# Three operands of VectorE's work in a 512-step recurrence are placed in PSUM instead of SBUF

## What is computed

```python
h = silu(cond @ W1.T + b1); gate = sigmoid(h @ W2.T + b2)
x = x + (x + x * gate)                 # layer 0: the transform and its inverse cancel, so x1 = x * (2 + gate)
# layer 1: a recurrence over the 512 steps
h_t = tanh(x1[:, t] @ Wx + b + h_{t-1} @ Wh);   x2[:, t] = x1[:, t] + h_t
# layer 2, from x2
f, i = sigmoid(x2 @ Wf.T + bf), sigmoid(x2 @ Wi.T + bi)
s = f + i + EPS;  f, i = f / s, i / s;  n = i * (x2 @ Wh2.T + bh)
# decays and cumulative sums of f and n over time, added to x2, give x3
# layer 3, from x3: for each batch a rank-8 correction (from cond) of a base matrix
out = x3 + x3 @ (x3-independent matrix of this batch)
```

## Time and profile before

| | us |
|---|---|
| runs | 1658.1, 1659.96, 1660.72; median 1659.96 |
| profiled execution, whole / span of the core | 1663.04 / 1661.2 |
| busy: PE, PEld | 1498.4 (90%), 1152.1 (69%) |
| busy: DVE, ACT, POOL | 1138.5 (69%), 556.5 (34%), 695.7 (42%) |

### The profile page before, as it was taken

How to read it: one execution, slowest core, us unless ns; L and a number is a source line. 1 busy time by engine, 2 the same in 40 slices (tenths; PEclk the granted TensorE clock), 3 DMA queues, 4 the chain that set the end, 5 groups by cost and what they waited for, 6 DMA issues and landing times. The chain is left out here.

```text
span 1661.2 us, 48465 instructions
## 1 busy us (share of the span) xinstructions
PE 1498.4 (90%) x20708; PEld 1152.1 (69%) x20708; DVE 1138.5 (69%) x2722; ACT 556.5 (34%) x1606; POOL 695.7 (42%) x540
## 2 busy tenths in 40 slices
PE   4768999999999999999999999999987976989998
PEld 3435777777777777777777777777776754666666
DVE  4223576776768676767677776768676778898884
ACT  3313333333333334333333333333323322232322
POOL 1314243434334444434343434434334447565563
PEclk9678999999999999999999999999997997999999
DMA  7263032424142323323232324142234367777672
GB/s 297 89 233 136 9 66 49 69 40 84 26 80 39 67 46 59 53 55 61 51 63 52 68 39 84 27 78 40 40 75 122 85 116 204 259 242 265 233 260 79
DMA packets 443114, 167.74 MB, mean 101 GB/s; under 512 B 407906, under 2 KB 411106, under 8 KB 439571
## 3 DMA queue, kind: packets, MB, share of 16 engines
q1 hardware_dynamic: 442898, 164.64, 39.5%
HBM read 96.25 MB, written 68.16 MB: 99 GB/s over the span
## 5 line engine op out<-in xcount | busy, mean ns | idle before, releaser
L437 PEld LDWEIGHTS recb<-hs,scanS 128*128 128x128 f16 x16384 | 444.7, 96 | 245.6 <-DVE hs L1087 237.2
L437 PE MATMUL recb<-hs,scanS 128*128 128x32 f16 x16384 | 495.8, 177 | 70.7 <-DVE hs L1087 68.7
L622 ACT ACTIVATE hs<-pre 128x64 f16<-128x64 f32 x512 | 131.6, 257 | 824.1 <-DVE pre L1079 824.1
L1077 DVE TENSOR_TENSOR pre<-recb,xw 128x64 f32<-128x64 f32 x512 | 114.7, 224 | 256.7 <-PE recb L437 255.3
L1087 DVE TENSOR_TENSOR hs<-hbuf,hs 128x64 f16<-128x64 f32 x512 | 170.1, 332 | 147.1 <-ACT hbuf L623 145.3
L947 DVE RECIPROCAL gates<-gates 128x64 f32<-128x64 f32 (+1 forms) x484 | 258.7, 555 | 0.4
L810 POOL TENSOR_TENSOR xt<-xt,hbuf 128x512 f32<-128x512 f32 x64 | 100.0, 1562 | 207.9 <-ACT hbuf L623 207.9
L798 POOL TENSOR_TENSOR x1lo<-xt,x1hi 128x512 fp32r<-128x512 f32 x62 | 87.7, 1416 | 219.1 <-ACT x1hi L629 211.5
L814 POOL TENSOR_TENSOR gates<-gates 128x512 f32<-128x512 f32 x64 | 83.1, 1299 | 174.0 <-DVE gates L947 174.0
L823 POOL TENSOR_TENSOR xt<-xt,pout 128x512 f32<-128x512 f32 x64 | 76.3, 1192 | 188.4 <-DVE pout L973 188.4
L1079 DVE TENSOR_TENSOR pre<-recb,pre 128x64 f32<-128x64 f32 x512 | 115.0, 225 | 17.6
(11 more groups left out here) (194 smaller groups left out, 2780.3 us busy)
## 6 DMA issues: line engine op xcount, KB each, us to landing
xt<-in_x SPq DMA_DIRECT2D x64, 256.0 KB, 3.4
g_d<-gst SPq DMA_DIRECT2D x64, 256.0 KB, 4.1
n_d<-nst SPq DMA_DIRECT2D x64, 256.0 KB, 3.0
x_d<-xt SPq DMA_DIRECT2D x64, 256.0 KB, 3.1
out<-gates SPq DMA_DIRECT2D x64, 256.0 KB, 2.5
xt<-x_d SPq DMA_DIRECT2D x28, 512.0 KB, 5.4
stage<-in_w SPq DMA_DIRECT2D x11, 1024.0 KB, 8.9
xt<-g_d SPq DMA_DIRECT2D x14, 512.0 KB, 7.1
```

Of the source, the lines that this page charges most:

```text
L437: last = nc.tensor.matmul(rec[:, m].rearrange("p a b -> p (a b)"), w[:, k, m * P:(m + 1) * P], hs[:, k].rearrange("p a b -> p (a b)"), sta ...
L622: nc.scalar.activation(hs[:, :, 0, :], pre[:], ACT.Tanh, scale=unscale).then_inc(s_h, 1)
L1077: nc.vector.tensor_tensor(pre0[:], rec[:, :, 0, :], xw[j % 2][:, t], ALU.add).then_inc(s_pre0, 1)
```

## The change

- The f32 copy of h of the current step gets a tile of its own in PSUM, `hps`: ScalarE writes tanh three times a step (hs high, hps, hbuf), and L1087 subtracts hs from hps. The wait for hbuf's ring stands behind the first two. GpSimd's add_h waits for hbuf by a new semaphore, `s_hb`. `pre` is double, so that the third tanh may still read it.
- `gate2` moves to PSUM. Both lie in the bank `konst`, whose ones (needed by the scans of the tail) are now written behind the recurrence instead of at the start.
- The sigmoid of the f gate is done twice, into `fbuf` and into `fps` (PSUM, bank `aux`), the second waiting for the `gate_sum` before it (`s_gs`); `gate_sum` reads fps.
- Four x1_gated of block 0 move from before L1087 to behind it. In block 15 the transposes to `aux` wait for s_gs, the copy `xa` out of `aux` comes at t = 3 instead of 8 on ScalarE, its low part on VectorE at t = 9 instead of 11, another (`xbl`) at t = 11 instead of 10.

```diff
-DVE_FIRST_EARLY = {m + 1: [("x11", m)] for m in range(C)}
-DVE_FIRST_LATE = {3: [("hgT",)], 15: [("x1", 0)], 18: [("x1", 1)], 21: [("x1", 2)], 24: [("x1", 3)]}
+DVE_FIRST_LATE = {1: [("x11", 0)], 2: [("x11", 1)], 3: [("hgT",), ("x11", 2)], 4: [("x11", 3)], 15: [("x1", 0)], 18: [("x1", 1)], 21: [("x1", 2)], 24: [("x1", 3)]}
...
-        pre0, pre = sb("pre0", [P, C, B]), sb("pre", [P, C, B])
-        gate2, h0wh = sb("gate2", [P, C, B]), sb("h0wh", [P, C, B])
+        pre0, pre = sb("pre0", [P, C, B]), [sb(f"pre{e + 1}", [P, C, B]) for e in range(2)]
+        h0wh = sb("h0wh", [P, C, B])
...
+        hps, gate2 = (konst[:, e * C * B:(e + 1) * C * B].rearrange("p (c b) -> p c b", c=C) for e in range(2))
+        fps = aux[:]
...
                     if j == NBLK - 1 and t == 2:
                         pe.wait_ge(d_xar, 16)
+                        pe.wait_ge(s_gs, C * (j - 1))
...
                 act.wait_ge(s_pre, TS * j + t + 1)
+                nc.scalar.activation(hs[:, :, 0, :], pre[t % 2][:], ACT.Tanh, scale=unscale).then_inc(s_h, 1)
+                nc.scalar.activation(hps, pre[t % 2][:], ACT.Tanh, scale=unscale).then_inc(s_h, 1)
                 if t % OCT == 0 and o >= RING:
                     act.wait_ge(s_x2, o - RING + 1)
-                nc.scalar.activation(hs[:, :, 0, :], pre[:], ACT.Tanh, scale=unscale).then_inc(s_h, 1)
-                nc.scalar.activation(hbuf[:, t % (RING * OCT)], pre[:], ACT.Tanh, scale=unscale).then_inc(s_h, 1)
+                nc.scalar.activation(hbuf[:, t % (RING * OCT)], pre[t % 2][:], ACT.Tanh, scale=unscale).then_inc(s_hb, 1)
...
-                nc.scalar.activation((fbuf if kind == "f" else ibuf)[:, m % 2, :], bank[n % C][:], ACT.Sigmoid,
-                                     bias=bias[kind][:, m:m + 1]).then_inc(emptied(kind), 1)
+                if kind == "i":
+                    nc.scalar.activation(ibuf[:, m % 2, :], bank[n % C][:], ACT.Sigmoid, bias=bias["i"][:, m:m + 1]).then_inc(s_is, 1)
+                else:
+                    nc.scalar.activation(fbuf[:, m % 2, :], bank[n % C][:], ACT.Sigmoid, bias=bias["f"][:, m:m + 1])
+                    act.wait_ge(s_gs, C * b + m) if C * b + m else act.wait_ge(s_lr, C)
+                    if b == NBLK - 2 and m == 0:
+                        act.wait_ge(s_xal, 1)
+                    nc.scalar.activation(fps, bank[n % C][:], ACT.Sigmoid, bias=bias["f"][:, m:m + 1]).then_inc(s_fs, 1)
...
-                            elif m == 3:
+                            elif m == 0:
                                 act.wait_ge(s_xat, 1)
...
-                pool.wait_ge(s_h, 2 * (TS * j + OCT * (s + 1)))
+                pool.wait_ge(s_hb, TS * j + OCT * (s + 1))
...
-                nc.vector.scalar_tensor_tensor(rbuf[:, m % 2, :], fbuf[:, m % 2, :], EPS2, ibuf[:, m % 2, :], ALU.add, ALU.add).then_inc(s_gs, 1)
+                nc.vector.scalar_tensor_tensor(rbuf[:, m % 2, :], fps, EPS2, ibuf[:, m % 2, :], ALU.add, ALU.add).then_inc(s_gs, 1)
...
-            nc.vector.memset(konst[:], 1.0).then_inc(s_one2, 1)
...
-                    nc.vector.tensor_tensor(pre[:], rec[:, :, 1, :], pre0[:], ALU.add).then_inc(s_pre, 1)
-                    if j == 0:
-                        for item in DVE_FIRST_EARLY.get(t, []):
-                            first_work(item)
-                    else:
+                    nc.vector.tensor_tensor(pre[t % 2][:], rec[:, :, 1, :], pre0[:], ALU.add).then_inc(s_pre, 1)
+                    if j:
                         for item in DVE_EARLY.get(t, []):
                             work(j, t, item)
                     dve.wait_ge(s_h, 2 * (TS * j + t) + 2)
-                    nc.vector.tensor_tensor(hs[:, :, 1, :], hbuf[:, t % (RING * OCT)], hs[:, :, 0, :], ALU.subtract).then_inc(s_hs, 1)
+                    nc.vector.tensor_tensor(hs[:, :, 1, :], hps, hs[:, :, 0, :], ALU.subtract).then_inc(s_hs, 1)
...
             last = NBLK - 1
+            dve.wait_ge(s_hs, TS * NBLK + 1)
+            nc.vector.memset(konst[:], 1.0).then_inc(s_one2, 1)
```

More of the change, by code:

```diff
@@ L161, in build @@
                                     "s_hyp s_lr s_h0").split())
-        (s_x1, s_x1h, s_x1l, s_xp, s_xw, s_rec, s_pre0, s_pre, s_h, s_hs, s_x2, s_x2h, s_x2l, s_lowd, s_f, s_i, s_c, s_fs, s_is, s_gs, s_r, s_fr,
+        (s_x1, s_x1h, s_x1l, s_xp, s_xw, s_rec, s_pre0, s_pre, s_h, s_hb, s_hs, s_x2, s_x2h, s_x2l, s_lowd, s_f, s_i, s_c, s_fs, s_is, s_gs, s_r, s_fr,
          s_in, s_g, s_n, s_zero, s_car, s_P, s_X) = (
-            sem("r_" + s) for s in ("s_x1 s_x1h s_x1l s_xp s_xw s_rec s_pre0 s_pre s_h s_hs s_x2 s_x2h s_x2l s_lowd s_f s_i s_c s_fs s_is s_gs s_r s_fr "
+            sem("r_" + s) for s in ("s_x1 s_x1h s_x1l s_xp s_xw s_rec s_pre0 s_pre s_h s_hb s_hs s_x2 s_x2h s_x2l s_lowd s_f s_i s_c s_fs s_is s_gs s_r s_fr "
                                     "s_in s_g s_n s_zero s_car s_P s_X").split())
@@ L1037, in _ @@
             dve.wait_ge(s_turn, 2)
-            nc.vector.tensor_scalar(gate2[:], by_batch, 2.0, None, ALU.add).then_inc(s_turned, 1)
+            nc.vector.tensor_scalar(gate2, by_batch, 2.0, None, ALU.add).then_inc(s_turned, 1)
             dve.wait_ge(s_turned, 2)
@@ L1100, in _ @@
                         nc.vector.memset(gst[:, :, :, 0], 0.0).then_inc(s_zero, 1)
-                    if j == NBLK - 1 and t == 10:
+                    if j == NBLK - 1 and t == 11:
                         dve.wait_ge(s_xbh, 1)
                         nc.vector.tensor_tensor(xbl.bitcast(F32R), xbraw, xbh, ALU.subtract).then_inc(s_xbl, 1)
-                    if j == NBLK - 1 and t == 11:
+                    if j == NBLK - 1 and t == 9:
                         dve.wait_ge(s_xah, 1)
```

## The result

The changed kernel takes 1588.2 us (median of 4, 1587.56 to 1589.18) against 1660.0 before: ratio 0.9565, 95% interval 0.9552 to 0.9579, 71.8 us less. Forecast were 1593 us and a range of 1586 to 1611. The profiled execution of the new kernel took 1587.56 us over a span of 1585.7, that of the old one 1663.04, so the two profiles differ by 75.5, a little more than the medians; the old one stood 3 us above its median.

A forecast was written before the change was run, and what follows sets the result against it. PE was taken to bound ordinary steps at 2.29 us, the chain having 0.05 to spare. Gains of 57.7 + 4.4 + 3.9 + 1.0 + 0.8 = 67.8, rounded to 67, gave 1660 - 67 = 1593 us; range 1586 to 1611.

The forecast's parts named there:

- rival 4: Start of the kernel and its first two blocks pass everything on: 5 to 7 us more gain, 1586 to 1588, chance 0.13.
- the head: Before the first step: the first two x1_gated get faster, 1.0 us gained, taken from 0 to 1.7.
- blocks 0 and 1: First two blocks: stalls partly hidden by PE's reduced clock and DMA waits; 3.9 us gained, between 0 and 8.8.
- blocks 2 to 15: Recurrence with steps at 2.29 us: blocks 2 to 14 gain 57.7 us, block 15 gains 4.4.
- PE's floor of 2.29 us: Ordinary recurrence steps: PE sets 2.29 us, the VectorE and ScalarE chain has 0.05 us to spare.
- the signs: What the new profile should show; here, PE's weight loads idle before recb about 54 us less.
- The second SBUF operand waits for GpSimd's running instruction: L1087 in the recurrence: with hps in PSUM its stalls under GpSimd instructions go, 54 us of excess.
- gate_sum from fps removes its stalls: Steps 17 and 23 of a block: with one PSUM operand, stalls of 0.6 to 0.8 us of the path go.
- The unseen price: ScalarE's write to PSUM and its visibility to VectorE: taken as 0, bounded by 0.1 us, at most 25 us in all.
- The rule against the change: VectorE's fixed part is 58 cycles from SBUF, 120 from PSUM: some 65 ns more, leaving a gain of some 60 us.
- ScalarE's added work is hidden: Third tanh and second f sigmoid: ScalarE's load a block goes from 28.19 to 38.7 of 73.5 us, hidden by idle time.
- Tail: After the recurrence: last chunk's gate_sum 0.69 instead of 1.75 us, hbuf at most 0.24 later; net 0.8 us gained.

The follow-up runs named there:

- all three in SBUF: The changed kernel with hps, gate2 and gate_sum's operand (fbuf instead of fps) back in SBUF: 1649.75 us, ratio 0.9948 to the kernel before.
- the pair with hbuf first: The changed kernel with hbuf written before hps: 1624.0 us; the same with gate_sum also reading fbuf in SBUF: 1633.6 us.

## Why the prediction was right, and where it was not

Measured were 1588.2 us. That is inside the range, but just below the 1589 to 1598 that had 0.60, next to rival 4 (1586 to 1588, 0.13): by the two profiles the head gave 4.5 us more than was taken for it, blocks 0 and 1 2.3 more. So blocks 2 to 15 came out as added up, and the terms around them were too small.

**PE's floor of 2.29 us** held. The sum over the blocks from it was off by 0.5 us in 57.7. It was tested from both sides: 0.15 us on the chain cost 0.06 a step, two fill matmuls less gave 0.08. The reading that made it possible was the 0.10 against 0.05 us between the subtraction's end and PE's start, in the earlier trace rows; the column of idle time names L1087 as the releaser in both. That the sum came so near is partly luck: the last section shows steps bound by PE in another pattern, by which the same blocks would have gained 62.7. The wait of PE's weight loads fell by 66 us where the signs said about 54; they had counted the subtraction's stalls and not gate_sum's. These stood in the same wait: with all three in SBUF, where gate_sum's stall in step 23 is gone and the subtraction's are all there, the wait is 9 us shorter than before (228.0 against 237.2).

**The second SBUF operand waits for GpSimd's running instruction**: shown. With hps moved to SBUF alone the stalls return, with the same GpSimd instructions above them. SBUF — State Buffer, Who interferes with whom, in the Trainium skill, says so: a VectorE instruction with two SBUF inputs and a GpSimd one that reads SBUF exclude each other, and the one that starts first has the ports for its whole length. The traces agree, down to who waits when the starts are 0.04 us apart.

**gate_sum from fps removes its stalls**: here, this step named the wrong cause. An operand in PSUM does keep gate_sum from waiting where GpSimd starts first (0.68 against 1.78 in step 17 with hps in SBUF; 9.7 us with hbuf first). But in the changed kernel GpSimd isn't first: the stalls did go, and the pace gave their sum rightly, but they would have gone with gate_sum left in SBUF. In step 23 they went because hbuf, and by it add_h, comes 0.15 us later; in step 17 because the subtraction no longer stalls. I had looked at operands and not at the order of the two starts, 832.97 and 833.11. The kernel with all in SBUF, expected at the old time and 9.3 us below it, and the pair with hbuf first show it.

**The unseen price**, a ScalarE write to PSUM, was taken as 0 with up to 0.1 us above. It is 30 ns below. ScalarE: Activation LUTs, Step-by-step: what each stage is for, in the Trainium skill, calls PSUM the quicker destination; 210 against 240 ns agrees. Filled steps gained nothing by it, as PE is the floor, but the cover did; a step without fill went from 2.31 to 2.27 (steps 4 to 7 of block 15), which the sum had at nothing.

**The rule against the change** in the Trainium skill (VectorE: DVE Perf Modes, on the TRN2 errata), by the prediction's estimate 65 ns more for a PSUM source, isn't seen for these two-operand forms: 224 ns with hps in PSUM, 226 with it in SBUF.

**ScalarE's added work is hidden**: right. Without the second sigmoid the time is the same, and the tanh costs only if it stands before hps.

**Head**: the size was off, 1.0 taken from a bound of 0 to 1.7, about 3.6 measured over ten profiles, beside a scatter of 2 us. Of this 1.7 is accounted for: from the start of GpSimd's first split (L837, now L846) to the end of its last it is 7.70 or 7.71 us in the three profiles with gate2 in SBUF and 5.93 to 5.97 in the other seven. That is the upper bound, by the mechanism that the prediction named for it (GpSimd's own instructions are shortened as well). The other 1.9 us are open. In the changed kernel's profile GpSimd's two pauses around the all-reduce, in which the trace shows it waiting for nothing, are shorter too, 6.3 and 6.8 us instead of 8.2 and 7.7; but over the ten profiles the pauses of the two groups overlap (the first 7.1 to 8.2 with gate2 in SBUF, 6.0 to 7.6 without), so it isn't shown that they depend on gate2.

**Blocks 0 and 1** gave 6.2, 3.9 taken of at most 8.8. The bound and its reason were both off. The trace of before has 0.2 us of the subtraction's stalls in block 0 and 2.4 in block 1, against 3.6 in most blocks behind them, and no gate_sum in block 0: the stalls were not hidden there, most of them did not exist. Block 1 gained 3.3 us; block 0 gained 2.9, far more than its stalls. Of the 2.9, a few hundredths a step come from the faster tanh and from x1_gated behind the subtraction (steps 1 and 2 of block 0 take 2.35 before, 2.31 with all three in SBUF, 2.27 or 2.28 as changed); where the rest comes from isn't shown.

**Tail**: 2.1 against 0.8, within what the ten profiles scatter (339.3 to 342.1 us).

## What to carry to other kernels

Look for VectorE instructions on the critical loop whose longest duration is far above the median, and see what GpSimd runs above them: one operand in PSUM takes such an instruction out of the conflict, and a spare ScalarE pays for the copy. Where both read SBUF, who starts first decides who waits, so shifting the release of the GpSimd instruction by a tenth of a microsecond may do as much as moving an operand; try the order before paying for the copy. And before counting a gain on a loop, compare the hand-over in its ordinary turn with the bare one: the difference is the cover, and what it hides can't be gained or lost.

## What was not expected of the hardware

Beside the waits, steps bound by PE come in two patterns: 2.29 in nearly every step, 73.39 us a block (the changed kernel's profile), or 2.26 and 2.30 in turn, 72.96 a block (the profiles with gate_sum from SBUF and without the second forget gate, spans of 1580.0 and 1582.0). Over the recurrence it makes 6 us, about the spread between runs of those kernels (1581.8 to 1591.5). In the profile of the kernel before both stand in one execution: 2.26 and 2.30 in turn through most of block 1, 2.29 in the ordinary steps behind step 9 of block 9. What chooses the pattern is open.
